# Two-layer graph network on one core: six slots for whole adjacency tiles and three split pairs, input chunks and the first row's loads at other places

## Reference, cut to what matters

```python
# layer 0
x_norm = layernorm(x, g_in, b_in)
y_soft = softmax(x_norm @ Wn + bn + gumbel)
gate = hard one-hot + y_soft - y_soft, column 1
view2 = (adj * gate[:, None] * gate[None, :]) @ x_norm
fusion = sigmoid(concat(x_norm, view2) @ Wg + bg)
fused = fusion * (x_norm @ W1 + b1) + (1 - fusion) * (view2 @ W2 + b2)
x = layernorm(x + layernorm(fused + x, g_out, b_out))
# layer 1, hyperbolic
mv = mobius_matvec(weight, x)
h = proj(mobius_add(proj(mv), proj(expmap0(bias))))
s = adj @ logmap0(h)
x = layernorm(x + expmap0(relu(logmap0(proj(expmap0(s))))))
```

## Time and profile before

| | |
|---|---|
| time, median of 3 runs | 954.12 us (953.48 to 954.53) |
| profiled execution: its time, its span | 953.25 us, 951.0 us |
| PE busy | 912.3 us (96%) |
| DVE, ACT, POOL busy | 793.5 (83%), 682.2 (72%), 232.8 us (24%) |
| granted PE clock, mean | 0.991 |
| DMA read and written, mean rate | 271.44 MB, 9.46 MB, 295 GB/s |
| A tile loads | 243, 6.1 us each from issue to landing (median) |
| the chain that ended last | PE 59%, DVE 23%, POOL 5%, ACT 5%, DMA 4% |

### The profile page before, as it was taken

How to read it: one execution, slowest core, us unless ns; L and a number is a source line. 1 busy time by engine, 2 the same in 40 slices (tenths; PEclk the granted TensorE clock), 3 DMA queues, 4 the chain that set the end, 5 groups by cost and what they waited for, 6 DMA issues and landing times.

```text
span 951.0 us, 12683 instructions
## 1 busy us (share of the span) xinstructions
PE 912.3 (96%) x4086; PEld 718.2 (76%) x4086; DVE 793.5 (83%) x1791; ACT 682.2 (72%) x1222; POOL 232.8 (24%) x201
## 2 busy tenths in 40 slices
PE   8998998999999999999999999998999999999993
PEld 4555786777888788888888888886777878778772
DVE  5577889999989799789686776779899998989886
ACT  6766787877767676757566465566879979789873
POOL 2210211112121211101020110201100755485473
PEclk9999999999999999999999999999999999999997
DMA  7989698988979686958576575766899999999980
GB/s 261 405 277 346 262 367 283 333 297 308 326 262 323 228 304 228 337 191 306 184 283 232 187 266 177 255 233 224 310 349 377 390 389 414 363 402 388 421 326 33
DMA packets 51824, 281.71 MB, mean 296 GB/s; under 512 B 6528, under 2 KB 8496, under 8 KB 20656
## 3 DMA queue, kind: packets, MB, share of 16 engines
q1 hardware_dynamic: 45936, 270.67, 76.6%
q10 hardware_dynamic: 5824, 10.25, 3.0%
HBM read 271.44 MB, written 9.46 MB: 295 GB/s over the span
## 4 chain that ended last, share of the span: by engine, by line
PE 59%; DVE 23%; POOL 5%; ACT 5%; DMA 4%; issue 3%; POOLq 0%; ACTq 0%; DVEq 0%
PE PS L1046 17%; PE PS L1048 17%; PE PS L1047 17%; DVE AL L771 5%; DVE XGL L771 5%; DVE XTL L771 3%; POOL r_rs L455 2%; PE PS L1149 2%; DVE BS L720 2%; DMA XR<-in_x_dram 2%; PE PS L1044 1%; DMA PART<-in_x_dram 1%; DMA A<-in_adjT_dram 1%; PE PS L1159 1%; DVE MV L724 1%
## 5 line engine op out<-in xcount | busy, mean ns | idle before, releaser
L771 DVE TENSOR_TENSOR AL<-A,AH 128x1024 fp32r<-128x1024 f32 x247 | 294.3, 1219 | 37.3 <-ACT AH L570 36.4
L570 ACT ACTIVATE AH<-A 128x1024 fp32r<-128x1024 f32 x247 | 252.8, 1057 | 95.7 <-PE PS L1048 86.7
L1046 PE MATMUL PS<-AH,XGH 128*128 128x512 f32 x344 | 138.9, 404 | 4.0 <-DVE AL L771 4.0
L1048 PE MATMUL PS<-AH,XGL 128*128 128x512 f32 x344 | 134.2, 390 | 0.0
L771 DVE TENSOR_TENSOR XGL<-A,XGH 128x1024 fp32r<-128x1024 f32 x113 | 132.3, 1217 | 2.2 <-ACT XGH L570 1.9
L1047 PE MATMUL PS<-AL,XGH 128*128 128x512 f32 x344 | 133.9, 389 | 0.0
L570 ACT ACTIVATE XGH<-A 128x1024 fp32r<-128x1024 f32 x113 | 112.7, 1055 | 10.8 <-DMA A<-in_adjT_dram 9.1
L1046 PE MATMUL PS<-AH,XTH 128*128 128x512 f32 x290 | 115.0, 397 | 4.2 <-DVE AL L771 4.2
L1048 PE MATMUL PS<-AH,XTL 128*128 128x512 f32 x290 | 113.4, 391 | 0.0
L1047 PE MATMUL PS<-AL,XTH 128*128 128x512 f32 x290 | 113.3, 391 | 0.0
L771 DVE TENSOR_TENSOR XTL<-A,XTH 128x1024 fp32r<-128x1024 f32 x92 | 108.8, 1219 | 4.0 <-ACT XTH L570 3.9
(11 more groups left out here) (260 smaller groups left out, 1589.6 us busy)
## 6 DMA issues: line engine op xcount, KB each, us to landing
A<-in_adjT_dram SPq DMA_DIRECT2D x243, 1024.0 KB, 6.1
x_scratch<-X SPq DMA_DIRECT2D x12, 256.0 KB, 5.8
GB<-gate_scratch SPq DMA_DIRECT2D x11, 256.0 KB, 3.5
XNT<-xnt_scratch SPq DMA_DIRECT2D x11, 256.0 KB, 3.9
XR<-in_x_dram SPq DMA_DIRECT2D x11, 256.0 KB, 4.7
PART<-in_x_dram ACTq DMA_DIRECT2D x6, 256.0 KB, 9.8
xnt_scratch<-XNT ACTq DMA_DIRECT2D x4, 256.0 KB, 7.4
xnt_scratch<-X1T ACTq DMA_DIRECT2D x4, 256.0 KB, 8.6
```

What stands on the lines that cost most here:

```text
L570: a.activation(high(m), A[:, n % RING, h * HW:(h + 1) * HW], ACT.Copy).then_inc(S["hi"], 1)
L771: v.tensor_tensor(low(m), A[:, n % RING, h * HW:(h + 1) * HW], high(m).bitcast(F32), ALU.subtract).then_inc(S["lo"], 1)
L1046: p.matmul(acc, hi[:, st], high(m)[:, mv], start=start, stop=False)
L1048: return p.matmul(acc, lo[:, st], high(m)[:, mv], start=False, stop=stop)
```

## The change

`RING` goes from 5 to 6 and `SPLITS` from 4 to 3. A slot takes 8 KB of each partition, and a pair 8 KB. So 7, 5 and 3 areas serve rows 1 to 5, 6 to 9, and 10 and 11, and 9 serve the second layer; the load of tile n waits for tile n-6. On ACT's queue, chunk 6 of x is loaded after the normalization of chunk 1 and chunk 7 after that of chunk 2, and step k of the loop loads chunk k+8. `load_first_front` is cut in two: at m = 25 the loads of `XNT` and `XR`, which wait for the stores of the chunks, and at m = 27 that of `GB`, which waits for the store of the gates.

```diff
-RING = 5
-SPLITS = 4
+RING = 6
+SPLITS = 3
...
-            def load_first_front():
+            def load_first_gates():
                 act.wait_ge(S["gate_stored"], 16)
+                act.dma_start(GB[:, :], gate_dram[0:1, :].partition_broadcast(P)).then_inc(S["epi_in"], 16)
+
+            def load_first_rows():
                 for i in range(3):
                     act.wait_ge(S[f"xnt_stored{i}"], 16 * (NCH // 3))
-                act.dma_start(GB[:, :], gate_dram[0:1, :].partition_broadcast(P)).then_inc(S["epi_in"], 16)
                 act.dma_start(XNT[:, :], xnt_dram[0:P, :]).then_inc(S["epi_in"], 16)
                 act.dma_start(XR[:, :], x[0:P, :]).then_inc(S["epi_in"], 16)
...
             normalize(1)
+            load_x(6)
             gate_exp(0)
...
             normalize(2)
+            load_x(7)
             gate_exp(1)
...
-                if k + 6 < NCH:
-                    load_x(k + 6)
+                if k + 8 < NCH:
+                    load_x(k + 8)
...
-                    load_first_front()
+                    load_first_rows()
+                if m == 2 * NCH + 3:
+                    load_first_gates()
```

## The result

| | before | after |
|---|---|---|
| median of the runs | 953.8 us (950.83 to 954.53, 4 runs) | 963.1 us (961.88 to 964.42, 4 runs) |
| profiled execution: time, span | 953.25, 951.0 us | 962.35, 958.6 us |
| PE busy; mean clock | 912.3 us; 0.991 | 914.7 us; 0.989 |

The median of before is of the three executions known at the forecast (954.12) and a fourth. The ratio is 1.0098, with a 95% interval of 1.0072 to 1.0125. The forecast was 958.2 with a range of 951.8 to 963.0: the direction was right, but the loss is 9.3 us where 4.1 were forecast, and the median lies just above the range. The span grew by 7.6 us; another 1.5 us of the profiled execution's 9.1 lie outside its span (3.75 instead of 2.25 us), which no view of the profile explains.

The account below looks back on a forecast made before the run. PE, busy 96% of the span, was taken as the bound. Gains of 6.4 us against losses of 8.8 and 1.7 for the clock gave net +4.1 on 954.12: 958.2 us, range 951.8 to 963.0.

Parts of the forecast that it names:

- Chunks of x: Opening, row 0: earlier loads take away DVE's waits for chunks 6 and 9; gain 3.0 us, ends 0 and 3.7.
- The rival that the store of chunk 1 would be pushed back: Opening: that store comes as late as chunk 6 came sooner, so the chunks win nothing; 961.2 us, chance 0.15.
- the 2 us of the sum by it: Opening: by ring order chunk 6's load delays the store behind it, taking 2 us off the 3.7 us gain.
- First row's loads: First row: splits of halves 26 and 27 come before the gates' store lands, `l0` starts sooner; gain 3.4 us.
- The slow stretch: First row: 3.4 us at half clock behind PE's 2.40 us wait, 1.7 us of work lost, likely to go.
- Sixth slot, nothing: SP starts each load one tile earlier; the second layer has nothing to relieve, so no gain.
- Row 6: 6 areas become 5, delaying the fusion and x1; loss 5.5 us, and 1.7 for another stretch at half clock.
- the two waits named: Row 6: PE waits 3.8 us for half 158's low part, then 2.9 us more for x1 before its transposes.
- Row 11: 3 areas instead of 4, delaying the fusion and x1; loss 2.4 us, ends 0 and 3.8.
- the two places named: Row 11: PE's low part wanted when half 270 ends, 1.05 us late; transposes of x1, 1.3 us late.
- Row 10 and the second layer's opening: Splits start later with one pair fewer, at small margins; losses 0.3 and 0.2 us.
- Sum: Whole kernel: gains 6.4 us, losses 8.8 us and 1.7 for the clock; net +4.1 us.

Follow-up runs that it names:

- experiment 4: Kernel before the change (RING 5, SPLITS 4, chunks at their old places) with only the first row's loads apart: 952.19 us, ratio 0.9991.
- experiment 5: As experiment 4, with SP holding tile 17 and all later tiles until the first row's three loads have landed: 949.79 us, ratio 0.995.
- experiment 6: Changed kernel with x1 of rows up to 6 in front of the split of half 163 in ACT's stream: 956.27 us, ratio 1.0013.
- experiment 3: Kernel before the change (RING 5, SPLITS 4) with only the x chunks loaded earlier: 949.56 us, ratio 0.996.
- experiment 11: RING 5, SPLITS 4, both moves of loads, tile 17 and later held until the first row's three loads landed: 946.72 us, ratio 0.9932.
- experiment 7: Kernel before the change with SPLITS 3 alone (RING 5), all loads at their old places: 967.79 us, ratio 1.0141.
- experiment 12: Changed kernel with x1 of rows up to 6 one half earlier, first row's gate product and `l0` three halves later: 957.9 us, ratio 1.0055.
- experiment 1: Kernel before the change with RING 6 and SPLITS 3 alone, all loads at their old places: 967.79 us, ratio 1.0166.

## Why the prediction was right in direction and wrong in size

- **Chunks of x**: -3.0 forecast, -3.5 measured. The rival that the store of chunk 1 would be pushed back fell: chunk 6 took 5.7 us from its earlier issue at 10.8 us, not 13.4, and that store, issued at 13.8 us, took 12.7, not 13.6. Part of the load went into the gap in which the DMA engines had been little busy: 253 GB/s in 14 to 17 us, where it was 151 before. The ring order that the Trainium skill states ("DMA: Bandwidth & Descriptors", "Queues, rings and completion order") isn't contradicted, but the 2 us of the sum by it did not show.
- **First row's loads: the step that failed.** The forecast was that GB "lands at 84.9 at the latest", from loads and store of that tensor that took 3.4 to 6.5 us, so -3.4 us. It took 8.8 us, 2.3 beyond my upper end, because earlier splits free slots and SP fills the DMA engines with tiles (experiments 4 and 5). I had counted the earlier splits as the gain and not followed what they start. The 85.7 to 86.0 us for the start of `l0` are counted in the times of the trace before; with the 3.5 us that the opening won, `l0` should have started at 82.2 to 82.5. It started at 85.00, which looks close to the number and is some 2.6 us late: only 0.8 of its 4.3 us come from this move. The slow stretch, which I took to be gone, came behind PE's wait before `l0` and cost the other 1.6 or so. The step was +0.8 instead of -3.4, so 4.2 of the 5.2 us by which the result exceeds the forecast are this step. How far this step moves by chance shows in experiment 6: its trace has the late GB without the slow stretch, and its step was -0.9.
- **Sixth slot, nothing**: right. Five and six slots with three pairs have ratios whose intervals overlap (1.0141 and 1.0166).
- **Row 6**: +7.2 forecast with the clock, +6.6 measured, by the two waits named and with one slow stretch of 3.4 us. The mechanism was right; the first wait grew by 1.75 us and not by 2.6. In the two kernels with the loads at their old places it was 9.3 and 9.5, for the clock.
- **Row 11**: 2.4 forecast, 2.7 measured, at the two places named.
- **Row 10 and the second layer's opening**: mis-sized, 0.3 and 0.2 forecast, 1.0 and 0.9 measured. Later in the second layer 1.2 us come back, most of it near half 410, where the trace before has a wait of 0.68 us for a low part (823.76 us) and the changed kernel none. Experiments 3 and 11, with five slots and four pairs, win about as much there, so it is no gain of the sixth slot.
- **Sum**: -3.5 + 0.8 + 0.2 + 6.6 + 1.0 + 2.7 + 0.9 - 1.2 = 7.5 us of span, against 4.1. The last 1.5 us outside the span stay open. The four runs of the changed kernel have 2.0 to 3.8 us there; of all 28 runs of the kernels with six slots six have more than 3.0, and no run of the others has more than 2.5.

## What to carry to other kernels

If a wait is taken from an in-order engine, ask what that engine's earlier work starts, in the DMA queues first: here freed slots started 1 MB loads whose products PE took only some 20 us later, beside the one load for which DVE and PE waited, and holding them back was worth more than the move itself (0.4% against 0.1%). A wait taken away at one place can come back at another: here covering PE's idle time in front of a round trip through DRAM won nothing. A pair of buffers less does not cost the same everywhere but in the rows where an epilogue step stands behind a split; the cure can be one place in the order.

## What the runs showed of the hardware

- The clock of PE fell from 2.4 to 1.2 GHz for 3.4 us behind waits of 2.2 to 3.9 us, but not always: the same wait of 3.30 us before `l0` had a slow stretch behind it in the changed kernel and none in experiment 6, where the step was 1.7 us cheaper. In three kernels (experiments 7, 11 and 12) it was also low at 14 to 18 us, where PE had waited 0.5 us at most in the 5 us before. Row 6 with the same two waits had 3.4 us at the low clock in the changed kernel and 10.2 in two others, a difference of 2.8 us in time.
- The same 256 KB load from `gate_scratch` into `GB` took 5.6 and 6.5 us where tiles were held back. With the loads at their old places it took 6.5 us before the change, where SP started no tile for 4.8 us behind it, and 6.0, 7.5 and 7.9 us in experiments 3, 1 and 7. In the eight other kernels with the gates' load behind the splits it took 8.2 to 9.3 us, and in all of them two 1 MB loads were issued on SP's queue within 4.3 us behind it. So later loads on another queue can slow an earlier one.
- A load of 256 KB on ACT's queue took 5.7 us issued at 10.8 us and, in the same trace, 15.3 issued at 14.4; before the change one issued at 18.4 took 13.4. What fills the DMA engines in between was not tried.
